# A two-layer kernel: where the softmax reciprocals are spread, where outer products are kept, and which ticks hold projections and norms

## The reference, cut to what matters

```python
xn = _layernorm(x)
s = attention(xn, Wq, Wk, Wv, Wo, bo)      # 16 heads of 64, causal softmax
g = _silu(ffn(xn, ...))                    # shared FFN + the best one of 8 experts
x = x + s * g
xn = _layernorm(x)
s = linear_attention(xn, ...)              # phi = elu + 1, 16 heads of 8
g = _silu(local_transformer(xn, ...))      # 2 layers, 8 heads of 64, window 64, GEGLU
x = x + s * g
# linear_attention:
kv_cum = jnp.cumsum(k[..., :, None] * v[..., None, :], axis=2)
k_cum  = jnp.cumsum(k, axis=2)
out = einsum(q, kv_cum) / (einsum(q, k_cum)[..., None] + EPS)
```

## Time and profile before

| what | us |
|---|---|
| median of 3 runs | 2106.64 (2105.45 to 2107.7) |
| the profiled execution's own time | 2113.86 |
| its span | 2112.1 |
| PE busy | 1783.7 (84%) |
| DVE busy | 1255.7 (59%) |
| ACT busy | 1187.6 (56%) |
| POOL busy | 895.2 (42%) |
| granted TensorE clock, mean | 0.922 |

### The profile page before, as it was taken

The page is one execution under the profiler, slowest core; times in us unless marked ns, Lnnn a source line. Parts: engine busy times, 40 slices in busy tenths (PEclk is TensorE's granted clock), DMA queues, the critical chain, the costliest instruction groups (busy, mean ns, idle before and its releaser), DMA issues.

```text
span 2112.1 us, 38035 instructions
## 1 busy us (share of the span) xinstructions
PE 1783.7 (84%) x12532; PEld 1147.1 (54%) x12532; DVE 1255.7 (59%) x4179; ACT 1187.6 (56%) x3527; POOL 895.2 (42%) x1025
## 2 busy tenths in 40 slices
PE   6679989997989889987989889987989798685876
PEld 4358754663565456654465456554565455363554
DVE  4434447556666556656766556656766656867653
ACT  2444547655656665666666565566566565553643
POOL 2633216523643245423553255414653255647510
PEclk9889999999999989999999999999999997787978
DMA  8146500000000000000000000000000000000000
GB/s 234 45 157 208 189 16 5 8 1 1 6 2 16 1 1 6 17 1 1 6 1 16 1 1 7 16 1 1 6 2 11 1 6 1 1 6 0 1 1 11
DMA packets 49725, 53.49 MB, mean 25 GB/s; under 512 B 6386, under 2 KB 42236, under 8 KB 49532
## 3 DMA queue, kind: packets, MB, share of 16 engines
q0 software_dynamic: 7808, 27.79, 4.0%
q1 hardware_dynamic: 41724, 23.26, 3.9%
HBM read 41.60 MB, written 9.44 MB: 24 GB/s over the span
## 4 chain that ended last, share of the span: by engine, by line
PE 46%; DVE 12%; issue 10%; ACT 7%; POOL 7%; DVEq 0%; ACTq 0%; POOLq 0%
PE ps L650 5%; PE ps L608 4%; PE ps L588 4%; PE ps L547 4%; PE ps L725 3%; PE ps L567 3%; PE ps L632 3%; PE ps L767 2%; PE ps L776 2%; PE ps L769 2%; PE ps L622 2%; POOL xn L308 2%; POOL big L1447 2%; DVE p L1033 2%; POOL big L1446 1%
## 5 line engine op out<-in xcount | busy, mean ns | idle before, releaser
L1333 POOL COPY rdx<-rden 128x256 f32<-128x256 f32 x256 | 99.5, 418 | 599.9 <-DVE rden L1050 574.9
L1033 DVE CUSTOM_DVE_ANT_0 p<-ps,mask 128x128 f32<-128x128 f32 (+1 forms) x512 | 152.2, 353 | 249.8 <-PE ps L580 215.3
L1033 DVE CUSTOM_DVE_ANT_0 p<-ps,mask,nrq 128x128 f32<-128x128 f32 x512 | 149.0, 347 | 204.1 <-PE ps L576 203.4
L588 PE MATMUL ps<-ident,p 128*128 128x128 f32 x1280 | 221.4, 297 | 26.8 <-ACT p L865 23.9
L865 ACT ACTIVATE p<-p,nmax 128x128 f32<-128x128 f32 (+1 forms) x512 | 226.4, 442 | 0.0
L725 PE MATMUL ps<-wqkv,hT 128*128 128x512 f32 x384 | 197.4, 623 | 27.9 <-ACT big L944 27.7
L864 ACT ACTIVATE p<-p,nmax 128x128 f32<-128x128 f32 x512 | 200.3, 391 | 34.5 <-DVE nmax L1033 34.0
L879 ACT ACTIVATE pt<-ps 128x384 f32<-128x384 f32 (+1 forms) x256 | 111.7, 436 | 185.2 <-PE ps L588 184.6
L588 PEld LDWEIGHTS ps<-ident,p 128*128 128x128 f32 x1280 | 143.8, 147 | 107.0 <-issue 89.2
L1446 POOL TENSOR_TENSOR big<-big,rots 128x512 f32<-128x512 f32 x64 | 99.6, 1556 | 206.0 <-ACT big L944 206.0
L557 PE MATMUL ps<-ident,big 128*128 128x128 f32 x512 | 90.9, 317 | 93.3 <-DVE big L1228 47.6
(11 more groups left out here) (251 smaller groups left out, 4207.7 us busy)
## 6 DMA issues: line engine op xcount, KB each, us to landing
slots_in<-xn SPq DMA_DIRECT2D x1, 2560.0 KB, 14.0
v<-slots_in SPq DMA_DIRECT2D x20, 128.0 KB, 4.6
slots_out<-v SPq DMA_DIRECT2D x20, 128.0 KB, 1.9
big<-in_x SPq DMA_DIRECT2D x4, 512.0 KB, 6.1
x<-in_x SPq DMA_DIRECT2D x8, 256.0 KB, 3.0
out_x<-x SPq DMA_DIRECT2D x8, 256.0 KB, 2.3
wqkv<-in_wqkv SPq DMA_DIRECT2D x2, 768.0 KB
xn<-in_x SPq DMA_DIRECT2D x6, 256.0 KB, 3.2
```

What stands on the lines that cost most here:

```text
L588: last = nc.tensor.transpose(bank[:, j * P:(j + 1) * P], c.p[:, u % 4, j * P:(j + 1) * P], c.ident[:, :])
L1033: last = V.tensor_tensor_reduce(out=c.p[:, u % 4, a:b], in0=bank[:, a:b], in1=mask, scale=scale, scalar=3e38, op0=ALU.add, op1=ALU.min, ac ...
```

## The change

1. **Reciprocals.** `expand` on POOL goes. PE turns rden (128x8) itself with one transpose, one tick earlier, ahead of `values`; ACT copies the 8x128 result to rdT, ahead of the exponentials of its tick. On SP a new step `spread`, the first in its tick, stores the 4 KB of rdT to DRAM, waits until they have landed, waits until the pair two before is scaled, and loads them back with two DMAs that repeat each row for 64 partitions (128 KB of rT each). rT has two buffers now. DVE's `scaled` stays in its tick and waits for the two loads. SP's order in a tick is then `spread`, `xs`, `ed`, `xload`, `xres`, `fin`, as they fall due.
2. **Outer products.** The second sequence's have a place of their own: the upper half of `big` that holds q and k (free once the last keys are transposed), or, for the last two blocks, the merged tile w0 of wq, wk and wv. They stand in one tick, l0+5, behind the first sequence's third part. The first's parts stand at l0+1, 2, 5, 6; the second's stay at l0+9 to 12.
3. **Keys over their norm.** All 4 tiles on DVE; POOL's stage goes.
4. **Other ticks.** `ln1` and `ln1n` of blocks 1 to 6, 8 ticks earlier. For blocks from 3 on `xload`, `xn`, `xnT` stand 14, 14 and 12 ticks earlier, and v, cut by tile, goes to ticks f0-11 and f0-10 (first half, two tiles each) and f0-1 and f0+7 (second half), f0 being the block's first step; before, 4 tiles stood in f0-2 and 4 in the tick 3 before the second half. `ffn` of blocks 3 to 6 stands in ticks 145 to 147 of the period shown (before 150 to 152), `down0` goes from 153 to 152, `r` from 151 to 150, `comb` stays in 153, `wo` of the second half goes from 148 to 151.

The diff, cut; first the plan, then PE, ACT, DVE, POOL and SP in this order:

```diff
-            self.put(a, "ln1", b)
-            self.put(a + 1, "ln1n", b)
+            self.put(a - (8 if 0 < b < LAST else 0), "ln1", b)
+            self.put(a - (7 if 0 < b < LAST else -1), "ln1n", b)
...
-            for t, at in enumerate((-1, 0, 6, 7)):
-                self.put(l0 + at, "kv", b, t)
-            for n in range(2 * LPARTS):
-                at = l0 + 1 + n + 4 * (n >= LPARTS)
+            for t in range(2):
+                self.put(l0 - 1 + t, "kv", b, t)
+            for n, at in enumerate((1, 2, 5, 6, 9, 10, 11, 12)):
+                self.put(l0 + at, "cum", b, n // LPARTS, n % LPARTS)
+                self.put(l0 + at + 1, "sum", b, n // LPARTS, n % LPARTS)
+                if n == 2:
+                    for t in range(2, TILES):
+                        self.put(l0 + at, "kv", b, t)
...
+            held.append((f0 - 5, f0 - 3) if b < XRING else (f0 - 19, f0 - 15))
...
-            if b:
-                self.put(f0 - 2, "v", b, 0)
-            self.put(f1 - 3, "v", b, 1)
+            for t in range(TILES):
+                if b:
+                    self.put(f0 - (2 if b < XRING else 11 - t // 2), "v", b, 0, t)
+                self.put(f1 - 3 if b < XRING else f0 - 1 if t < 2 else f0 + 7, "v", b, 1, t)
+            late = 4 if XRING <= b < LAST else 0
             for half in range(2):
-                self.put(self.end[(0, b, half, PAIRS - 1)] + 4, "wo", 0, b, half)
-            c = max(self.end[(0, b, 1, PAIRS - 1)] + 4, e_end + 3)
+                self.put(self.end[(0, b, half, PAIRS - 1)] + 4 + (late - 1 if late and half else 0), "wo", 0, b, half)
+            c = max(self.end[(0, b, 1, PAIRS - 1)] + 4, e_end + 3) + late
...
-                self.put(c - 3 + ch, "ffn", b, ch)
+                self.put(c - 3 - late + ch, "ffn", b, ch)
...
-            self.put(c, "comb", b)
+            self.put(c + (late > 0), "comb", b)
...
     def merge(pair):
         bank = mm_bank("m", pair)
-        pe.wait_ge(c.rdx_ready, pair + 1)
-        for t in range(TILES):
-            last = nc.tensor.transpose(bank[:, t * P:(t + 1) * P], c.rdx[:, t * P:(t + 1) * P], c.ident[:, :])
-        last.then_inc(c.mm_full, 1)
+        pe.wait_ge(c.rden_ready, pair + 1)
+        nc.tensor.transpose(bank[0:8, 0:P], c.rden[:, :], c.ident[:, :]).then_inc(c.mm_full, 1)
...
+        if (st := plan.step(tick - 1)) and st.s:
+            merge(st.pair)
         if st := plan.step(tick - 2):
             values(st)
-            if st.s == 1:
-                merge(st.pair)
...
     def merge(pair):
+        bank = mm_bank("m", pair)
         if pair:
-            act.wait_ge(c.o_done, o.done("o", pair - 1))
-        evacuate(c.rT[:, :], "m", pair)
+            act.wait_ge(c.rd_stored, 16 * pair)
+        A(c.rdT[:, :], bank[0:8, 0:P], ACT.Copy).then_inc(c.mm_done, 1)
...
+        if (st := plan.step(tick - 1)) and st.s:
+            merge(st.pair)
         if plan.step(tick):
             exps(plan.step(tick))
-        if (st := plan.step(tick - 2)) and st.s == 1:
-            merge(st.pair)
...
     def scaled(st):
         dve.wait_ge(c.pv_done, st.n + 1)
-        dve.wait_ge(c.mm_done, mm.done("m", st.pair))
-        TT(c.attT[st.kind][:, st.i, :], c.o_ps[o.slot("o", st.pair)][:, :], c.rT[:, :], ALU.mult)\
+        dve.wait_ge(c.rT_loaded[st.pair % 2], 32 * (st.pair // 2 + 1))
+        TT(c.attT[st.kind][:, st.i, :], c.o_ps[o.slot("o", st.pair)][:, :], c.rT[st.pair % 2][:, :], ALU.mult)\
             .then_inc(c.o_done, 1)
...
-        for t in range(KN_VECTOR):
+        for t in range(TILES):
             k_over_norm(V, c, t).then_inc(c.kn_ready, 1)
...
+        elif t == 2 and b < LAST - 1:
+            pool.wait_ge(c.mm_full, last_keys(plan, mm, plan.turn[(b, 0)]))
         elif t == 2:
-            pool.wait_ge(c.mm_full, mm.full("cum", b, 0, LPARTS - 1, 0))
-            pool.wait_ge(c.prod_ready, 4 * LPARTS * b + 2 * LPARTS)
+            pool.wait_ge(c.mm_full, mm.full("k", last_pair(plan, 0, LAST, 1)))
...
     for tick in range(plan.length):
-        if (st := plan.step(tick - 1)) and st.s == 1:
-            expand(st.pair)
...
+    def spread(st):
+        sp.wait_ge(c.mm_done, mm.done("m", st.pair))
+        sp.dma_start(dram.rd[st.pair].rearrange("(u q) -> u q", q=P), c.rdT[:, :]).then_inc(c.rd_stored, 16)
+        sp.wait_ge(c.rd_stored, 16 * (st.pair + 1))
+        if st.pair >= 2:
+            sp.wait_ge(c.o_done, o.done("o", st.pair - 2))
+        for h in range(2):
+            f = HD * h
+            sp.dma_start(c.rT[st.pair % 2][f:f + HD, :], dram.rd[st.pair][h * TOK:(h + 1) * TOK].partition_broadcast(HD))\
+                .then_inc(c.rT_loaded[st.pair % 2], 16)
```

More of the change, by code:

```diff
@@ L237, in lay_out @@
             self.put(l0 + 18, "s1", b)
-        held, shared = [(self.first[(0, b, 0, 0)] - 5, self.first[(0, b, 0, 0)] - 3) for b in range(2, BLOCKS)], {}
+        held, shared = [], {}
+        for b in range(2, BLOCKS):
+            f0 = self.first[(0, b, 0, 0)]
+            held.append((f0 - 5, f0 - 3) if b < XRING else (f0 - 19, f0 - 15))
         for b in range(BLOCKS):
@@ L326, in buffers @@
     c.router = sb("router", [P, EXPERTS])
[L327 to L328 removed]
+    w0 = sb("w0", [P, 3 * INNER0])
+    c.wqk, c.wv = [w0[:, i * INNER0:(i + 1) * INNER0] for i in range(2)], w0[:, 2 * INNER0:3 * INNER0]
     c.wo0 = sb("wo0", [P, 2 * PAIRS, P])
@@ L489, in count_units @@
                 whitened[seg[0] == "ln2n"] += 1
-        if (st := plan.step(tick - 2)) and st.s:
+        if (st := plan.step(tick - 1)) and st.s:
             mm.add(("m", st.pair))
@@ L847, in shifted, with values_of_tokens @@
         A(two(c.hT[HD:P, :])[:, :, 1:SEQ], two(bank[HD:P, :])[:, :, 0:SEQ - 1], ACT.Copy).then_inc(c.mm_done, 1)
-    def values_of_tokens(b, half):
-        for t in range(TILES):
-            evacuate(c.v0[:, half, t, :], "v", b, half, t)
+    def values_of_tokens(b, half, t):
+        evacuate(c.v0[:, half, t, :], "v", b, half, t, 0)
     def produce(which, st):
@@ L981, in scalar @@
         evacuate(c.xnT[:, i, :] if i < 2 else c.xrT[i % 2], "rT", i)
-    values_of_tokens(0, 0)
+    for t in range(TILES):
+        values_of_tokens(0, 0, t)
     produce(0, plan.step(0))
@@ L1324, in gpsimd @@
     link = Chain(pool, c.pool_chain)
-    def expand(pair):
-        pool.wait_ge(c.rden_ready, pair + 1)
-        if pair:
-            pool.wait_ge(c.mm_full, mm.full("m", pair - 1))
-        rd = c.rden[:, :].rearrange("p (s h i) -> p s i h", s=2, h=2)
-        for sq in range(2):
-            out = c.rdx[:, sq * SEQ:(sq + 1) * SEQ].rearrange("p (i h d) -> p i h d", i=2, h=2)
-            last = G.tensor_copy(out, rd[:, sq, :, :].unsqueeze(3).to_broadcast([P, 2, 2, HD]))
-        last.then_inc(c.rdx_ready, 1)
     def scatter(j):
@@ L1544, in store @@
         sp.dma_start(x_out[:, TILES * b:TILES * (b + 1), :], c.x[:, b % XRING, :, :]).then_inc(c.stored[b % XRING], 16)
+    def spread(st):
[8 more added lines that the diff above has]
+                .then_inc(c.rT_loaded[st.pair % 2], 16)
     stage = {"xs": load_slots, "ed": store_slots, "xload": xload, "xres": xres, "fin": store}
     for tick in range(plan.length):
+        if (st := plan.step(tick - 1)) and st.s:
+            spread(st)
         for seg in plan.side.get(tick, ()):
```

75 lines of the change are left out of this document (35 added, 40 removed), and 2 rows, old and new, of the table USES.

## The result

The changed kernel took 2150.95 us (median of 4 runs, 2146.68 to 2156.83) against 2107.17 for the kernel before (4 runs, 2105.45 to 2109.18): a ratio of 1.0209 [1.0183, 1.0236]. It is 2.1% slower; the interval holds 2% too and lies far from no change. The forecast was 2041, with a range up to 2085. The profiled execution took 2150.15, its span 2148.3 and its mean granted clock 0.905 (0.922 before).

What follows compares the result with a forecast made beforehand. PE was taken as the nearest bound, at 46% of the end time, with gains only from single stalls. Five periods of -12.4 (-62), fill +7 and tail -10 gave -65: 2041 us, range 2010 to 2085.

Steps and rivals of the forecast that it cites:

- Keys: PE's stalls at the keys: all four tiles on DVE and v's matmuls in the gaps, -2.3 us a period.
- The second norm: PE's wait for `ln2n`: DVE's tiny steps no longer run beside POOL's product or copies, -2.6 us a period.
- Refilled gaps: Rival: each stall removed uncovers another engine's work, leaving -6 us a period and 2079 us; chance 0.12.
- no effect: Rival: POOL only waited for DVE, so taking its work away does nothing; 2100 to 2110 us; chance 0.04.
- the trip is late: Slower rival: DVE at L1055 waits for two loads run one behind the other, 4.6 us each; 2181 us; chance 0.08.
- Fill: Start of the kernel (0 to 453.6): slot loads late behind `spread` and block 0's outer products, +7 us.
- Merges: One PE transpose of the reciprocals in place of four, with 3 of 16 ticks light: -3.5 us a period.
- reciprocals on the path everywhere: Rival: the earlier merge holds PE and ACT in most ticks, up to 54 us; 2085 us; chance 0.06.
- The trip through DRAM: Reciprocals stored and loaded back in 5.5 us, hidden except at the kernel's end: +2 us.
- xT: PE's wait of 1.59 us for xn ahead of xT goes, `ln1n` standing 8 ticks earlier: -1.6 us a period.
- v: v's matmuls leave one tick (-3.7 us), half returning in two ticks, half in key stalls; -2.4 us counted a period.
- Tail: Last stretch (1629 to 2112): keys, xT, POOL's relief and merges, less the end's +2: -10 us.

Runs made afterwards that it cites:

- one gate back: Changed kernel with one wait changed: POOL's first outer products of a block wait until DVE has divided its keys by their norms; 2110.79 us, 0.9966 of the kernel before.
- the run that reorders the two: Changed kernel with PE's transpose of the reciprocals behind the values and ACT's copy behind the exponentials; 2138.31 us, 1.0111 of the kernel before.
- the three orders mended: Changed kernel with outer products behind the keys, spread behind slot loads in ticks under 30, and merge behind values and exponentials; 2058.64 us, 0.9765 of the kernel before.

## Why the prediction was wrong, step by step

**The step that failed: "Keys".** It priced the division's move from POOL to DVE by its speed (-0.9, and 1.4 more on DVE), and "What bounds the kernel now" did the same for the copies: "Nobody waits for POOL's speed there. Removing them is worth little by itself." Both are right about speed. Neither asked what stood behind the two removed waits on POOL. It was the outer products, and DVE's inverse norms are issued at the moment they are let go. The six keys' ticks are 56 longer than before in the traces (9.3, 5.7 and four of 9.6 to 11.3). With one gate back they are 13 longer, so 43 of the 56 were this loss, and by the ratios the whole kernel gained 51. The other 13 are mostly the work that part 4 moved in. The row that would have told was the timeline of before: L1432 starts right behind L1333's end, although its own condition, the rotation, had been met 14 us earlier (the rotation's last instruction, L1228, ends at 808.85). "The second norm" had the same contention in view and counted it as a gain there alone; the idea that the freed products would go and do the same elsewhere is missing from the rivals. "Refilled gaps" and "no effect" say that a gain doesn't come, neither names this loss, and none of the rivals with 2150 in reach ("the trip is late") had this mechanism.

Of this, the Trainium skill, "SBUF — State Buffer", Who interferes with whom, says that the two engines share a port pair, and that whichever issues first holds it for its whole instruction while the other is blocked outright; the page says the last of VectorE's two-port modes. By that rule each small step would last up to the length of the POOL instruction beside it, and the trace agrees with 2.09 and 2.17 beside instructions of 2.2 and 2.65 beside one of 2.61. I had cited the section for relief. Its sharper sentence, about the whole instruction, was the one that bore on this change.

**"Fill": +7 forecast, +36 measured by the end of the expert stage and +52 by tick 63.** For the expert stage the mechanism was right, and the term mis-sized was the lateness: I took 1.9 for the store and up to 3 a tick in all. The store's own wait took 3.7 here, ACT's copy stands behind all of ACT's expert stages of the tick, and with the two loads' issue (1.09) the slot load left 8 to 10 later in its tick than in the kernel before. Of the 16 behind it, 9 are the keys' tick 45. My sign for it, PE's waits at L680 (L686 after) over 15, fired with 42.9, and moving the loads ahead gave 38 back.

**"Merges": -3.5 a period forecast.** The sign was wrong. I took 3 of 16 ticks as light. PE in fact waits for the reciprocal 46 times in the run, 73.4 us in all, against the 54 that I had named as the upper end. The rival "reciprocals on the path everywhere" was closest here: its sign (more than 20 us of that wait) fired. It is worth some 21 us by the run that reorders the two; set against the forecast's 65, it alone would have left a gain. With the order mended the light ticks are at zero, not yet at a gain.

**What held.** *The trip through DRAM*: 5.5 taken, 5.7 measured for the last pair, from the store's issue to `scaled` (timeline of the kernel after):

```profile
2108.42 0.27 SPq L1539 DMA_DIRECT2D spread<-sh  x1
2109.76 1.79 SPq L1545 DMA_DIRECT2D rT<-spread  x2
...
2114.10 0.69 DVE L1063 TENSOR_TENSOR attT<-ps,rT 128x512 f32<-128x512 f32 x1 [3.82 <-DMA rT<-spread]
```

DVE waited for the loads twice in the run, 4.2 us in all, 3.82 of that at the end (+2 forecast, +3 measured). The slower rival is refuted: two loads of 128 KB one behind the other didn't come near its 9.2. (From the figures of the Trainium skill, "SBUF — State Buffer", The DMA setup-cost knee, I had estimated 5.2; the measured 5.7 is what counts.) *The second norm*: its steps take 0.16 each now, and PE's wait of 4.58 is gone, but 2.49 of it came back as the wait for the reciprocal in the same ticks. *xT*: without a wait. *v*: -4.0 in the tick it left (forecast -3.7). *Keys' own stalls*: PE waits 3.62 where it waited 5.34, and no longer for the second half where it had waited 3.10, but those two ticks together gain 0.8 to 1.3, not 2.3. The matmuls of v that fill the gap run at a low clock, so the 1.4 that I took for the clock didn't come. The window behind the first stall in the kernel after:

```profile
1030.26:1039.00 8.74, 8.74 (x41) 5.43 (x41) 6.67 (x26) 3.50 (x10) 0.00 (x0) 0.66 0.01 3
```

PE is busy all the time there, at a granted 0.66, lower than the 0.70 of before. *Tail*: -6.9 against -10.

Taken together: with the three orders mended the kernel gains 2.35% (some 50 us) against the 3.1% (65 us) that the forecast summed. The sum was near for a kernel in which nothing is let go early and nothing stands in front of the slot loads. In the kernel as written three losses stand against it, 51, 38 and 21 by the single runs, 110 together. Mended at once they return 1.0209 - 0.9765 = 4.4%, or 94 us. That a part of them shares the same pauses would explain it, but isn't shown: the gap of 16 us is little more than the intervals of these ratios leave open.

**What stays open.** Of the 4 to 5 us that the keys' tick still costs, 3.4 are PE's own work in the tick looked at. What ends the 1.8 of added idle time was not settled: DVE's work there (rotation's end, norms, masks) seems to be the bound, and the run that moved `wo` out showed only that it isn't `wo` alone. Of the fill's +52, 7 lie between ticks 46 and 63 and weren't traced to a cause. How much of the keys' loss is the lower granted clock behind the long pause (0.92 in the period against 0.95 with the gate back) and how much is the pause wasn't measured apart.

## What to carry to other kernels

Before work is taken from an idle engine, list what is queued behind it there and what its waits held back: an engine that is 35% busy can still cost 2.4% by starting too early. A gate that comes for free with a piece of work has to be put back on purpose when the work goes, at the consumer's date and not at the earliest one. The same holds for a queue that issues DMAs: a step that waits for its own transfer belongs behind the loads that others need soon. And the part blamed for a slower kernel may be sound: the reciprocals through DRAM cost 3.6% put in as they stood, and with the three orders mended the kernel is 1.5% ahead of the one that keeps the copies (0.9765 against 0.9913).

## What the runs showed of the hardware that I had not expected

- A DVE instruction of 64 or even 4 elements per partition lasts until the POOL instruction beside it ends: 0.16 to 0.23 alone, 2.09 to 2.65 beside an outer product of 128x1152 on POOL (2.2 each) or the sum of two (2.61), with the two ends within 0.1 of each other. That goes for the int32 step with one input (L292: 0.20 to 2.09) as for those with two. In these rows it is not a slowdown by a share but a stop for the rest of the POOL instruction, so a chain of short steps suffers most. A larger one suffers too: the keys' four tiles took 7.29 beside POOL in the fill, 2.49 alone.
- A 4 KB store to DRAM with a wait behind it lets the next issue go after some 1.2 us in quiet stretches (1.34 in the last pair, start to start), and after 2.5 to 4.7 in the expert stage, where the slots' and the weights' transfers run.
- The granted clock went with the pauses: 0.92 in the period of the kernel after with its pauses of 9.9, 0.95 in the same period once they were 2.3.
